# Two PSUM banks in turn for the block stage's xb and y, and y's products ahead of act's transposition

## What is computed

```python
logits = xf @ Wg
top_w, top_i = jax.lax.top_k(logits, TOP_K)          # 2 of 8
top_w = jax.nn.softmax(top_w, axis=-1)
h = jnp.einsum('nc,ech->enh', xf, W1)                # 128 -> 256
g = jnp.einsum('nc,ech->enh', xf, W2)
y = jnp.einsum('enh,ehc->enc', jax.nn.silu(h) * g, W3)
out = jnp.einsum('enc,ne->nc', y, combine)
```

## Time and profile before

| what | us |
|---|---|
| median of 3 runs | 505.36 |
| the profiled execution, its own time | 504.81 |
| its span, first to last instruction | 502.9 |
| block stage, first transposition of xb to last wide product | 126.5 |
| PE busy in the span | 460.3 |
| DVE busy in the span | 387.8 |
| ACT busy in the span | 300.9 |

### The profile page before, as it was taken

The page is one execution under the profiler, slowest core; times in us unless marked ns, Lnnn a source line. Parts: engine busy times, 40 slices in busy tenths (PEclk is TensorE's granted clock), DMA queues, the critical chain, the costliest instruction groups (busy, mean ns, idle before and its releaser), DMA issues. The chain is left out here.

```text
span 502.9 us, 14460 instructions
## 1 busy us (share of the span) xinstructions
PE 460.3 (92%) x4462; PEld 373.9 (74%) x4462; DVE 387.8 (77%) x1684; ACT 300.9 (60%) x752; POOL 231.4 (46%) x320
## 2 busy tenths in 40 slices
PE   2478999999999999889999999989999999899997
PEld 1246877777777787677887887768888877777996
DVE  4557789999899878767688568767799986677973
ACT  2377877777777775455555665475535556453653
POOL 2322155666666445547300377543687871314420
PEclk9999999999999999999999999999999999999999
DMA  8801011111111110146664344220100221000011
GB/s 232 323 12 54 14 33 34 42 37 37 37 37 33 35 53 24 44 131 187 183 178 140 106 134 118 78 68 18 27 22 22 57 71 33 11 1 1 1 43 43
DMA packets 44126, 34.60 MB, mean 69 GB/s; under 512 B 5922, under 2 KB 40098, under 8 KB 43812
## 3 DMA queue, kind: packets, MB, share of 16 engines
q1 hardware_dynamic: 28884, 20.02, 13.1%
q0 software_dynamic: 4384, 8.93, 6.3%
q10 hardware_dynamic: 10800, 4.92, 3.5%
HBM read 21.85 MB, written 11.99 MB: 67 GB/s over the span
## 5 line engine op out<-in xcount | busy, mean ns | idle before, releaser
L473 POOL DMA_INDIRECT sent<-xr,rowu x60 | 59.0, 984 | 62.2 <-DVE rowu L1038 48.1
L489 POOL DMA_INDIRECT yg<-done,gidx x64 | 65.4, 1021 | 31.5 <-issue 15.6
L1257 DVE TENSOR_TENSOR act<-sil,bank 128x256 f32<-128x256 f32 x71 | 29.8, 420 | 26.8 <-ACT sil L693 25.7
L927 DVE TENSOR_REDUCE mx<-bank 128x8 f32<-128x512 f32 x64 | 41.1, 682 | 10.3 <-PE bank L1691 9.9
L455 POOL TENSOR_TENSOR ve<-mv,half 128x4 f32<-128x4 f32 (+1 forms) x40 | 8.8, 221 | 85.9 <-DVE mv L851 83.2
L693 ACT ACTIVATE sil<-bank 128x256 f32<-128x256 f32 x71 | 27.2, 383 | 35.3 <-PE bank L1864 34.4
L1880 PE MATMUL bank<-f0w_s,aT 128*128 x284 | 44.4, 279 | 0.8 <-DVE yb L1263 0.8
L634 ACT ACTIVATE Pr<-bank 128x512 f32<-128x512 f32 x64 | 34.7, 597 | 14.3 <-PE bank L1705 14.3
L640 ACT ACTIVATE PT<-bank 128x512 f32<-128x512 f32 x64 | 37.2, 609 | 4.5 <-PE bank L1654 4.1
L1691 PE MATMUL bank<-QK 64*64 64x256 f32 x512 | 36.7, 404 | 2.9 <-ACT QK L624 2.9
L1880 PEld LDWEIGHTS bank<-f0w_s,aT 128*128 128x128 f32 x284 | 37.2, 191 | 1.9 <-issue 1.2
(11 more groups left out here) (254 smaller groups left out, 1287.7 us busy)
## 6 DMA issues: line engine op xcount, KB each, us to landing
xb<-sent SPq DMA_DIRECT2D x71, 64.0 KB
done<-yb ACTq DMA_DIRECT2D x71, 64.0 KB
cT<-ctx_t_dram SPq DMA_DIRECT2D x16, 128.0 KB
f0w_s<-f_w_dram SPq DMA_DIRECT2D x1, 2048.0 KB, 10.5
Pr<-ctx_t_dram SPq DMA_DIRECT2D x8, 256.0 KB
QK<-ctx_tok_dram SPq DMA_DIRECT2D x8, 256.0 KB
out_dram<-xs SPq DMA_DIRECT2D x8, 256.0 KB, 2.3
xs<-x_dram SPq DMA_DIRECT2D x2, 512.0 KB, 6.8
```

The costliest lines, as they stand in the source:

```text
L473: nc.gpsimd.indirect_dma_start(sent, bass.IndirectOffsetOnAxis(ap=rowu[:, s, 2 * k + c:2 * k + c + 1], axis=0), rows[:, c, :], None).then_ ...
L489: nc.gpsimd.indirect_dma_start(yg[:, s, j, :], None, done[0:NG1 * P, :] if u < UG else done, bass.IndirectOffsetOnAxis(ap=gidx[:, s, j:j + ...
L927: nc.vector.tensor_reduce(mx[:, g, :], bank[SC_BANK[g]][:].rearrange("p (m k) -> p m k", k=L), AX, ALU.max).then_inc(S("a_max"), 1)
```

## The change

xb is transposed into bank 4 for even blocks and bank 7 for odd ones (up to block 61; then bank 4 alone), y is made in bank 2 for even blocks and bank 5 for odd ones (up to block 56; then bank 2 alone). `before(bank_of, t)` gives the number of the last block that used the same bank, so the waits of xb's transposition and of y's products reach two blocks back. The first two wide products wait for xbh, and only the third for xbl. PE makes y of block t-3 ahead of the transposition of act of block t-2, and ACT copies aT at the start of the step behind that transposition. Two waits are added before the next stage first writes banks 5 and 7.

```diff
+        def xb_bank(t):
+            return bank[7 if t % 2 and t < NB - 9 else 4]
+
+        def y_bank(t):
+            return bank[5 if t % 2 and t < NB - 14 else 2]
+
+        def before(bank_of, t):
+
+            return max((i + 1 for i in range(t) if bank_of(i) is bank_of(t)), default=0)
...
             def b_step(t, q, first, last):
 
                 k = q % 2
+                if first >= 3:
+                    a.wait_ge(S("b_at"), t - 2)
+                    if first >= 5:
+                        a.wait_ge(S("b_y"), t - 4)
+                    nc.scalar.activation(aT[:, 1 - k], bank[6][:, 0:2 * P].rearrange("p (j n) -> p j n", n=P), ACT.Copy).then_inc(S("b_ats"), 1)
                 if last >= 0:
                     a.wait_ge(S("b_xt"), t + 1)
-                    nc.scalar.activation(xbh[:, k, :], bank[4][:, 0:P], ACT.Copy).then_inc(S("b_xts"), 1)
+                    nc.scalar.activation(xbh[:, k, :], xb_bank(t)[:, 0:P], ACT.Copy).then_inc(S("b_xts"), 1)
...
-                if first >= 2 and last >= -2:
-                    a.wait_ge(S("b_at"), t - 1)
-                    if first >= 4:
-                        a.wait_ge(S("b_y"), t - 3)
-                    nc.scalar.activation(aT[:, k], bank[6][:, 0:2 * P].rearrange("p (j n) -> p j n", n=P), ACT.Copy).then_inc(S("b_ats"), 1)
...
                     pe.wait_ge(ld_b[q % 4], (t - q % 4) * 4 + 16)
-                    if first >= 1:
-                        pe.wait_ge(S("b_xls"), t)
-                    transposes("b_xt", bank[4], lambda c: xb[:, q % 4, :], 1)
+                    wait(pe, S("b_xls"), before(xb_bank, t))
+                    transposes("b_xt", xb_bank(t), lambda c: xb[:, q % 4, :], 1)
                 if first >= 1 and last >= -1:
                     e = expert(t, 1)
-                    pe.wait_ge(S("b_xls"), t)
                     high, low = (w[:, bass.ds(e, 1), :].rearrange("p e n -> p (e n)") for w in (f0w12_h, f0w12_l))
+                    pe.wait_ge(S("b_xts"), t)
                     mm(bank[1 - k][:], xbh[:, 1 - k, :], high, start=True, stop=False)
                     mm(bank[1 - k][:], xbh[:, 1 - k, :], low, start=False, stop=False)
+                    pe.wait_ge(S("b_xls"), t)
                     mm(bank[1 - k][:], xbl[:, 1 - k, :], high, start=False, stop=True).then_inc(S("b_hg"), 1)
...
+                if first >= 3:
+                    e = expert(t, 3)
+                    if first == 3:
+                        pe.wait_ge(S("a_x"), 1 + UA)
+                    wait(pe, S("b_ys"), before(y_bank, t - 3))
+                    pe.wait_ge(S("b_ats"), t - 2)
+                    for j in range(2):
+                        last_mm = mm(y_bank(t - 3)[:, 0:D], aT[:, 1 - k, j, :],
+                                     f0w3_s[:, bass.ds(e, 1), j, :].rearrange("p e n -> p (e n)"), start=j == 0, stop=j == 1)
+                    last_mm.then_inc(S("b_y"), 1)
                 if first >= 2 and last >= -2:
                     pe.wait_ge(S("b_act"), t - 1)
-                    if first >= 3:
-                        pe.wait_ge(S("b_ats"), t - 2)
                     transposes("b_at", bank[6], lambda c: act[:, k, P * c:P * (c + 1)], 2)
-                if first >= 3:
-                    e = expert(t, 3)
-                    pe.wait_ge(S("b_ats"), t - 2)
...
                 if t == NB - 10:
+                    pe.wait_ge(S("b_ys"), NB - 14)
                     c_xt(0, 0)
                 if t == NB - 8:
+                    pe.wait_ge(S("b_xls"), NB - 9)
                     c_s(0, 0)
```

More of the change, by code:

```diff
@@ L1251, in b_step @@
                     v.wait_ge(S("b_xts"), t + 1)
-                    nc.vector.tensor_tensor(xbl[:, k, :], bank[4][:, 0:P], xbh[:, k, :], ALU.subtract).then_inc(S("b_xls"), 1)
+                    nc.vector.tensor_tensor(xbl[:, k, :], xb_bank(t)[:, 0:P], xbh[:, k, :], ALU.subtract).then_inc(S("b_xls"), 1)
                 if first >= 1 and last >= -1:
@@ L1262, in b_step @@
                         v.wait_ge(st_b[slot], (t - (3 + slot)) * 4)
-                    nc.vector.tensor_copy(yb[:, slot, :], bank[2][:, 0:D]).then_inc(S("b_ys"), 1)
+                    nc.vector.tensor_copy(yb[:, slot, :], y_bank(t - 3)[:, 0:D]).then_inc(S("b_ys"), 1)
             def comb(u, k, a):
```

## The result

The changed kernel took 514.11 us (median of 4, 511.25 to 514.43) against 505.28 for the kernel before; the ratio is 1.0148, 95% interval 1.0109 to 1.0187. Forecast were 508.4 and a range up to 511.5. So the change makes the kernel slower by 1 to 1.5%, 5 to 9 us where 3 were forecast.

The account below looks back on a forecast made before the run. PE, with work in 460.3 of 502.9 us, was taken as the bound; -1.9 + 1.5 + 0.8 + 0.4 + 2.2 = +3.0 us gave 508.4 us, range 501.8 to 511.5.

Parts of the forecast that it names:

- The loop: Middle 48 steps: act's transposition, aT, y and back take 1.59 us a round against 1.47; +1.5 us.
- PE alone: Rival: the loop hides in the middle 48 steps, quiet steps stay 1.47 us; 502.1 us in all; chance 0.2.
- the late restart: Rival: PE's queue restarts late behind each aT; at 0.2 us, round 1.67, 4.9 us more, 513.3; chance 0.15.
- What the two xb banks remove: Block stage: PE's stalls on late xbl go; 17 and 19 late weight loads, 7.8 and 3.9 us.
- First 13 steps: Start of the blocks: PE idles 3.9 us, in part for xbl; half of it gained, -1.9 us.
- The late steps: Last steps of the blocks: e3 and xT ahead of aT, +0.8 us; four steps losing 0.11 each, +0.4.
- The last aT behind the exponentials: End of the blocks: last copy after the next stage's exponentials delays the last y and Pc's transposition, +2.2 us.
- the end is covered: Rival: the exponentials and last aT do not delay the next stage's chain; 506.2 us; chance 0.08.
- break-even of 1.59 a step: Middle steps: the whole change breaks even at 1.59 us a step instead of the forecast 1.65.

Follow-up runs that it names:

- e1_banks: Changed kernel with the old order of y and aT put back, two banks for xb and y and the split wait kept: 500.54 us, ratio 0.9861.
- e6_copy_back: Changed kernel with only the copy aT put back to the end of its step on ScalarE: 507.42 us, ratio 1.0026.
- e10_no_split: Kernel before with two banks for xb only; all three wide products wait for xbl as before: 503.93 us, ratio 0.9943.
- e7_xb_bank: Kernel before with two banks for xb and the split wait, y in bank 2 alone: 500.25 us, ratio 0.9864.
- e8_filler_both: Changed kernel with six more filler products ahead of the last y, the six behind it kept: 510.0 us, ratio 1.0065.
- e2_order: Changed kernel with one bank each for xb and y again, the new order kept: 513.33 us, ratio 1.0128.
- e9_late_old_order: Old order with two xb banks and split wait; block 69's copy aT moved behind e3, block 70's behind the exponentials: 504.11 us, ratio 0.9951.
- e5_changed_again: Changed kernel measured a second time, not edited, giving the second profile after the change: 511.48 us, ratio 1.0107.
- e4_late_copy: Kernel before with only block 70's copy aT moved behind the four exponentials: 509.47 us, ratio 1.0054.
- e3_filler_ahead: Changed kernel with the six filler products moved from behind the last y to ahead of it: 508.73 us, ratio 1.0035.

## Why the prediction was wrong, point by point

The step that failed is one that the sum does not have: the granted clock behind PE's idle time at the end of the blocks, put at nothing, which cost 1.6 to 2.8 us. The first measurement lies a further 3.1 us up by a second stretch at 1.2 GHz, ahead of the blocks, whose cause stays open. Of the terms that the sum does have, two came in another size. The points one by one:

**The loop (+1.5 forecast, +1.33 to +1.46 measured): right, with its mechanism.** 1.59 us a round, 1.69 and 1.79 in the steps with more register instructions, y at 0.71, aT's end 0.25 ahead of y, the middle in 79.3 to 79.4. `e1_banks` and `e6_copy_back` show that PE's order makes it. The 0.10 us that y takes longer was right, but not its reason, that y's weights are a fresh copy. The last y of the earlier trace rows took 0.71 with a copy that had ended 1.11 us earlier, and one of the changed kernel took 0.61 with a copy of 0.40 us before:

```profile
332.98 0.38 ACT L698 ACTIVATE aT<-bank 128x256 f32<-128x256 f32 x1
```
```profile
217.70 0.38 ACT L694 ACTIVATE aT<-bank 128x256 f32<-128x256 f32 x1 [0.89 <-PE bank L1657]
...
218.48 0.61 PE L1877 MATMUL bank<-f0w_s,aT 128*128 x4
```

The first y waited for yb, the second shows no wait: 0.71 goes with a y that had to wait, whatever it waited for. Of the rivals, PE alone is what the banks give without the order (quiet steps 1.47 to 1.48), and the late restart did not come.

**What the two xb banks remove: half right.** The stalled steps are gone, but `e10_no_split` shows that a bank without the split wait moves part of the stall to the wide product, and gives 2.2 of the 3.3 us in the middle and 0.6 of the 1.4 per cent in all; I had credited the bank. Line L1654 in the earlier trace rows is also that of every transposition, not of xb's alone, as I read it: of its 17 late weight loads 9 are xb's, 4.1 of the 7.8 us. The Trainium skill (Perfetto Trace Analysis, Matmuls) asks for rotating banks, so that the evacuation of one overlaps the next group's products; the runs agree (0.9943 with xb's second bank alone), and give more where the wait of the products behind is split as well (0.9864).

**First 13 steps (-1.9 forecast, -0.73 to -0.88 measured): the step failed by omission.** Banks and split alone give -1.57 (`e7_xb_bank`, 24.97), near the forecast; but the loop stands in these steps too, and I charged its price only from step 13 on: 0.7 to 0.8 us given back.

**The late steps (+1.2 forecast, +0.69 to +0.76 measured): mechanism right, size off.** e3 and xT ahead of aT cost 0.99 in block 63's step (0.8 forecast). The four steps that I let lose 0.11 each lost nothing: three of the steps are 0.11 to 0.14 shorter than before (block 61's 2.62 against 2.73, 67's 1.70 against 1.84, 70's 1.48 against 1.60) and one is longer by 0.13.

**The last aT behind the exponentials (+2.2 forecast, +2.10 measured at the upper clock): right.** The last y 5.40 behind the last wide product (5.5 forecast).

**The sum: +3.0 forecast, +3.35 measured by the same steps, and the time is 508.51 us where the clock stays up (`e8_filler_both`).** That the two are so near is in part luck: the first 13 steps came 1.0 short of their forecast, the late steps cost 0.4 less than theirs. What failed is what stood nowhere in the sum: the granted clock. I read 1.00 in the earlier trace rows and carried it over, although the sum itself put the last y 5.5 us behind the last wide product, with PE idle for some 3 us between them. That idle time brought a stretch at 1.2 GHz in all four profiles in which both last copies are late and the wait is not filled (after, after again, `e2_order`, `e9_late_old_order`), which costs another 1.6 to 2.8 us in the end of the blocks (10.27 and 11.48 against 8.67). The Trainium skill (TensorE: Matmul & The Clock Gate, Part 1) says that the engine's clock is gated down by default and that activity releases it. The runs agree in direction: 1.46 us of useless products at the place keep it at 2.4 GHz.

**The rest of the first measurement need not be the change's.** Its profile has the early stretch at 1.2 GHz as well (+3.1 us up to the blocks), which `e7_xb_bank` shows once in the same place and `e5_changed_again` does not. 508.5, with 1.6 to 2.8 for the end and 3.1 in executions with the early stretch, gives 510.1 to 514.4; measured were 511.09 to 514.43, and 516.01 in one execution, whose span was 511.4. That the early stretch came as often by chance in the executions after is not shown: only one of the first four was profiled, and the mean clock does not tell, since 511.25 and 514.42 us both had 0.990. The 1.3 us that the second profile loses behind Pc were not traced further.

**The end as a whole.** The rival "the end is covered" fell, and the break-even of 1.59 a step had the late end in it but not the clock: another 1.6 to 2.8 us.

A version better than both kernels is what the runs point to: two banks for xb with the split wait, and the old order, `e7_xb_bank` at 0.9864 or `e1_banks` at 0.9861.

## What to carry to other kernels

Before an engine's order is changed, follow the new order once round: a product that waits for a copy of the thing it now stands ahead of makes a loop, and that loop then sets the quiet step, with one bank or two. Where a sum puts TensorE idle for microseconds, add a term for the clock behind it, or put filler products into the wait. A second buffer pays in full only if the consumer's wait is split too (1.4 per cent here, against 0.6); otherwise part of the stall moves one instruction on.

## What the runs showed of the hardware

- The granted clock fell with PE busy for 2.22 us in 4.61, 2.22 in 5.34 and 2.11 in 4.43 us ahead of the fall (after, after again, `e9_late_old_order`), and stayed at 1.2 GHz for 6.83, 3.41 and 6.83 us with PE busy again for most of it. In `e4_late_copy`, with PE busy for 2.20 in 5.27 us, it stayed up.
- Stretches at 1.2 GHz away from the end of the blocks stand in profiles of kernels with either order: 10.24 us from 36.5 (after, `e7_xb_bank`), 3.41 us between 205 and 211 (`e1_banks`, `e3_filler_ahead`, `e4_late_copy`, `e10_no_split`) and 3.41 us between 367 and 377 (`e3_filler_ahead`, `e6_copy_back`, `e7_xb_bank`).
- The mean clock differs between executions of the kernel before: of its 56 executions in these comparisons with a recorded clock 13 had a mean of 1.000, at 504.38 to 505.99 us, and the five of the lowest mean, 0.987, took 508.3 to 508.85 us.
- y's two products take 0.61 us at 2.4 GHz where PE need not wait ahead of them, 0.71 where it must, and 1.22 at 1.2 GHz after a wait.
